# Attention scores computed a second time with keys on partitions, instead of transposing the exponentials

## The reference, cut to what matters

```python
q, k, v = (proj(Wq, bq), proj(Wk, bk), proj(Wv, bv))
scores = jnp.einsum('bhqd,bhkd->bhqk', q, k) / jnp.sqrt(jnp.float32(HD))
scores = scores + slopes[None, :, None, None] * distances[None, None, None, :]
scores = jnp.where(causal, scores, jnp.finfo(scores.dtype).min)
attn = jax.nn.softmax(scores, axis=-1)
ctx = jnp.einsum('bhqk,bhkd->bhqd', attn, v)
...
gate = jnp.einsum('bsh,ih->bsi', hidden_states, gate_w)
up = jnp.einsum('bsh,ih->bsi', hidden_states, up_w)
ffn = jnp.einsum('bsi,hi->bsh', silu(gate) * up, down_w)
out = x + (ctx @ Wo + bo) + ffn
```

## Time and profile before

| | us |
|---|---|
| device time, median of 3 runs (lowest, highest) | 875.54 (874.05, 877.53) |
| the profiled execution: its own time | 878.33 |
| the profiled execution: span of its instructions | 876.1 |
| TensorE busy | 712.3 (81%) |
| VectorE busy | 547.9 (63%) |
| ScalarE busy | 429.0 (49%) |
| GpSimd busy | 349.7 (40%) |

### The profile page before, as it was taken

How to read it: one execution, slowest core, us unless ns; L and a number is a source line. 1 busy time by engine, 2 the same in 40 slices (tenths; PEclk the granted TensorE clock), 3 DMA queues, 4 the chain that set the end, 5 groups by cost and what they waited for, 6 DMA issues and landing times. The chain is left out here.

```text
span 876.1 us, 15410 instructions
## 1 busy us (share of the span) xinstructions
PE 712.3 (81%) x4884; PEld 562.1 (64%) x4884; DVE 547.9 (63%) x1337; ACT 429.0 (49%) x961; POOL 349.7 (40%) x207
## 2 busy tenths in 40 slices
PE   5668878877788887798798778138896999999997
PEld 4556666665566665576576656026775888888886
DVE  5287879979779977969979884547532221321312
ACT  4257566657547756656856662124543233233331
POOL 2344434434334433435434441417314223524534
PEclk9878889999889998899999679657999999999999
DMA  7982374345375326365525941947435546524401
GB/s 243 216 191 38 86 149 117 44 79 88 85 192 74 48 50 118 77 170 73 74 51 119 232 171 64 328 130 241 112 117 166 164 130 214 168 73 132 144 1 49
DMA packets 53031, 109.90 MB, mean 125 GB/s; under 512 B 6360, under 2 KB 6616, under 8 KB 51416
## 3 DMA queue, kind: packets, MB, share of 16 engines
q1 hardware_dynamic: 52808, 108.82, 49.6%
q10 hardware_dynamic: 144, 0.07, 0.0%
HBM read 59.32 MB, written 25.17 MB: 96 GB/s over the span
## 5 line engine op out<-in xcount | busy, mean ns | idle before, releaser
L995 POOL TENSOR_TENSOR work<-work 128x1280 f16<-128x1280 f32 x64 | 168.1, 2626 | 263.1 <-DVE work L720 263.1
L908 ACT ACTIVATE work<-work,neg_max 128x128 f32<-128x128 f32 (+3 forms) x256 | 140.7, 551 | 183.6 <-DVE neg_max L713 183.6
L528 PE MATMUL bank<-ident,work 128*128 128x128 f16 x1280 | 115.1, 236 | 61.2 <-DVE work L727 56.6
L707 DVE CUSTOM_DVE_ANT_0 work<-bank,dist 128x128 f32<-128x128 f32 (+3 forms) x256 | 116.7, 488 | 67.3 <-PE bank L514 65.8
L1483 POOL TENSOR_TENSOR in_lo<-inner,in_hi 128x512 fp32r<-128x512 f32 x64 | 84.1, 1315 | 179.1 <-ACT in_hi L1386 179.1
L528 PEld LDWEIGHTS bank<-ident,work 128*128 128x128 f16 x1280 | 81.4, 106 | 108.4 <-DVE work L727 74.4
L1437 DVE TENSOR_TENSOR inner<-bank,silu 128x512 f32<-128x512 f32 x64 | 44.1, 689 | 134.3 <-ACT silu L1380 122.3
L1386 ACT CAST in_hi<-inner 128x512 fp32r<-128x512 f32 x64 | 39.7, 621 | 146.5 <-PE bank L1325 137.5
L917 ACT COPY work<-bank 128x768 f16<-128x768 f16 (+1 forms) x128 | 107.8, 891 | 2.8 <-PE bank L528 2.8
L514 PE MATMUL bank<-k_stack,q_stack 96*128 96x256 f32 (+2 forms) x256 | 80.8, 393 | 27.1 <-issue 9.4
L1323 PE MATMUL bank<-w_room,in_hi 128*128 128x512 f32 x256 | 100.4, 392 | 0.5 <-POOL in_lo L1483 0.5
(11 more groups left out here) (102 smaller groups left out, 1426.0 us busy)
## 6 DMA issues: line engine op xcount, KB each, us to landing
q_stack<-parts SPq DMA_DIRECT2D x48, 256.0 KB, 5.6
k_stack<-parts SPq DMA_DIRECT2D x48, 256.0 KB, 5.6
z<-xt_scratch SPq DMA_DIRECT2D x128, 88.0 KB
x_in<-x SPq DMA_DIRECT2D x32, 256.0 KB, 4.6
xt_scratch<-xt_room SPq DMA_DIRECT2D x8, 1024.0 KB, 6.5
xt_room<-xt_scratch SPq DMA_DIRECT2D x6, 1024.0 KB, 8.1
factor<-c_basis SPq DMA_DIRECT2D x5, 1024.0 KB, 10.9
taps<-windows SPq DMA_DIRECT2D x5, 1024.0 KB, 12.9
```

The lines of the kernel that those rows point to most:

```text
L528: mm = pe.transpose(pt_bank[i % 2][:, (part * n + k) * P:(part * n + k + 1) * P], probs16[:, s % 2, part, OFF[i] + k * P:OFF[i] + (k + 1) ...
L707: dve.tensor_tensor_reduce(probs[:, s % 2, OFF[i]:OFF[i] + n], score_bank[i % 2][:, 0:n], dist[:, S - n:S], 1.0, -3.4e38, ALU.add, ALU.max ...
L908: e = act.activation(tile, tile, ACT.Exp, bias=neg_max[:, s % 2, i:i + 1], scale=slope(s), accum_out=row_sum[:, s % 4, i:i + 1])
L995: pool.tensor_tensor(probs16[:, s % 2, 1, :], probs[:, s % 2, :], probs16[:, s % 2, 0, :], ALU.subtract).then_inc(lo_ready, 1)
```

## The change

The transposition of the exponentials is gone. Instead the scores are computed a second time with keys on partitions, so that their exponentials land transposed.

- VectorE's `bias_and_max` now keeps only the maxima (the biased scores go to a scratch tile `spill`). `negate_max`, VectorE's `probs_high` and both `take_turned` are removed.
- In the next step TensorE transposes the 128 x 4 maxima to 4 rows in the score bank (`turn_max`), ScalarE adds a shift and copies them to `max_rows` (`take_max`), and SP moves them as one row of 512 into row 97 (numbered from 1) of the head's `q_stack` (`load_max`). Rows 97 and 98 (`EDGE:ROWS`) of the stacks hold constants, set once by GpSimd at the start (two operations over 2 x 8 x 512) from a row of distances, so that the second product comes out as score + distance - maximum.
- Two steps after the first scores, `scores_t` computes the second ones in three units of 512, 384 and 384 columns (four float32r matmuls of 512, 384, 256 and 256 columns), each with a bfloat16 matmul of `ahead` by `ident16` of 128 columns that masks the diagonal block. ScalarE exponentiates from PSUM, three activations, no row sums; a step later it rounds to float16 (`probs_high`, now on ScalarE), GpSimd makes the rest, and `weigh_values` comes four steps after the scores. A value tile has two more columns that are one, so the product also holds the row sum.
- The stacks are rings of 8 heads. `stack` is per half of a group (two heads), four DMAs for each head: 8 for a half, 16 for a group, and now waits for both q and k first.
- The second scores of head s read a row that is there only after TensorE, ScalarE, SP and a DMA; and the second matmul of `scores` (i = 1) waits for `max_read`, since it writes the bank in which the maxima lie.
- The tables of units and turns are shifted by a step in places, and `load_early` is issued by ScalarE after step 12 of the last batch.

```diff
...
-OFF = [0, 128, 384, 768]
+ST_UNITS = 3
+ST_AT = [0, 512, 896]
+ST_COLS = [512, 384, 384]
+OFF = [0, 512, 896, 1152]
...
+RING = 8
+EDGE = 3 * HD
+ROWS = EDGE + 2
+ST_LAG, HALVE_LAG, AV_LAG = 2, 3, 4
...
-UNITS = {0: [("q", 1)], 1: [("k", 1)], 2: [("o", 0)], 3: [("o", 1)], 4: [("q", 2)], 5: [("k", 2)], 6: [("o", 2)],
+UNITS = {0: [("q", 1)], 1: [("k", 1)], 2: [("q", 2)], 3: [("o", 0)], 4: [("o", 1)], 5: [("k", 2)], 6: [("o", 2)],
...
-TURNS = {2: [("c", 3)], 7: [("c", 0)], 9: [("x", 0), ("x", 1)], 10: [("x", 2), ("x", 3)], 11: [("c", 1)],
-         15: [("c", 2)]}
...
-SPLITS = {13: [(0, 0)], 14: [(0, 1)], 1: [(0, 2)], 2: [(0, 3)], 4: [(1, 0)], 5: [(1, 1)], 6: [(1, 2)], 7: [(1, 3)]}
+TURNS = {0: [("c", 2)], 3: [("c", 3)], 8: [("c", 0)], 9: [("x", 0), ("x", 1)], 10: [("x", 2), ("x", 3)],
+         12: [("c", 1)]}
...
+                if h % 2 == 0 and i == 0:
+                    for m in range(2):
+                        pe.wait_ge(stacked[m][c % 2][h // 2], 2 * STACK * b + STACK * (c // 2 + 1))
...
+                if i == 1 and (later(b) or s >= 1):
+                    pe.wait_ge(max_read, H * b + s)
...
-            def turn_probs(b, s, i):
...
+            def turn_max(b, s):
+                pe.wait_ge(t_done, 64 * b + 4 * s + 4)
+                pe.transpose(score_bank[s % 2][0:QT, 0:P], row_max[:, s % 2, :], ident[:]).then_inc(max_full, 1)
+
+            def scores_t(b, s, u):
+                g = ST_UNITS * s + u
+                if u == 0:
...
-                    pe.wait_ge(hi_ready, H * b + s + 1)
-                    pe.wait_ge(lo_ready, H * b + s + 1)
-                if later(b) or 2 * s + i // 2 > 0:
-                    pe.wait_ge(pt_free[i % 2], 2 * (H * b + s) + i // 2)
-                n = i + 1
-                for part in range(2):
-                    for k in range(n):
-                        mm = pe.transpose(pt_bank[i % 2][:, (part * n + k) * P:(part * n + k + 1) * P],
...
+                    pe.wait_ge(max_ld[s % 2], 8 * H * b + 16 * (s // 2 + 1))
+                if later(b) or g >= 2:
+                    pe.wait_ge(p_ready, ST_UNITS * H * b + g - 1)
+                bank, slot = st_bank[g % 2], s % RING
+                if u == 2:
+                    pe.matmul(bank[:, P:3 * P], k_stack[:, slot, 3 * P:], q_stack[:, slot, 2 * P:], start=True,
+                              stop=False)
+                    pe.matmul(bank[:, 2 * P:3 * P], ahead[:], ident16[:], start=False, stop=True)
+                n = S - u * P
+                pe.matmul(bank[:, 0:n], k_stack[:, slot, u * P:(u + 1) * P], q_stack[:, slot, u * P:], start=True,
+                          stop=False)
+                pe.matmul(bank[:, 0:P], ahead[:], ident16[:], start=False, stop=True).then_inc(st_full, 1)
...
+                own, before, crossed, weighed = (back(b, s, n) for n in (0, 1, ST_LAG, AV_LAG))
...
+                early, rest = ([], units) if s == 4 else (units[:1], units[1:])
+                if before:
+                    turn_max(*before)
                 for i in range(2):
                     if own:
                         scores(b, s, i)
+                if crossed:
+                    scores_t(*crossed, 0)
                 for i in range(2):
                     if weighed:
                         weigh_values(*weighed, i)
...
-                for i in range(2, QT):
-                    if own:
-                        scores(b, s, i)
-                if turned:
-                    turn_probs(*turned, 0)
+                if own:
+                    scores(b, s, 2)
+                if crossed:
+                    scores_t(*crossed, 1)
+                if own:
+                    scores(b, s, 3)
                 for key in early:
                     unit(b, s, key, (2,))
-                if turned:
-                    turn_probs(*turned, 1)
+                if crossed:
+                    scores_t(*crossed, 2)
                 for i in range(2, QT):
                     if weighed:
                         weigh_values(*weighed, i)
-                for key in early if s != 2 else []:
+                for key in early if s != 3 else []:
                     unit(b, s, key, (3,))
-                for i in range(2, QT):
-                    if turned:
-                        turn_probs(*turned, i)
...
                 if (later(b) or s >= 2) and tiles[0] == 0:
-                    dve.wait_ge(lo_ready, H * b + s - 1)
...
-            def negate_max(b, s):
-                dve.wait_ge(t_done, 64 * b + 4 * s + 4)
-                dve.tensor_scalar(neg_max[:, s % 2, :], row_max[:, s % 2, :], -slope(s), None,
-                                  ALU.mult).then_inc(nm_ready, 1)
...
-            def probs_high(b, s):
-                dve.wait_ge(p_ready, H * b + s + 1)
-                if later(b) or s >= 2:
-                    dve.wait_ge(pt_full, 4 * (H * b + s - 1))
-                dve.tensor_copy(probs16[:, s % 2, 0, :], probs[:, s % 2, :]).then_inc(hi_ready, 1)
...
-            def take_turned(b, s, i):
-                n = 2 * (i + 1) * P
-                dve.wait_ge(pt_full, 4 * (H * b + s) + i + 1)
-                if i == 0 and (later(b) or s >= 2):
-                    dve.wait_ge(av_full, H * b + s - 1)
-                dve.tensor_copy(probs_t[:, s % 2, 2 * OFF[i]:2 * OFF[i] + n],
-                                pt_bank[i % 2][:, 0:n]).then_inc(pt_free[i % 2], 1)
...
+            def take_max(b, s):
+                act.wait_ge(max_full, H * b + s + 1)
...
+                if later(b) or s >= 2:
+                    act.wait_ge(max_ld[s % 2], 8 * H * b + 16 * (s // 2))
+                act.activation(max_rows[:, s % 2, :], score_bank[s % 2][0:QT, 0:P], ACT.Identity, bias=shift[:, 0:1],
+                               scale=1.0).then_inc(max_read, 1)
+
+            def probs_high(b, s):
+                act.wait_ge(p_ready, ST_UNITS * H * b + ST_UNITS * (s + 1))
+                if later(b) or s >= 2:
+                    act.wait_ge(av_full, H * b + s - 1)
+                act.copy(probs16[:, s % 2, 0, :], probs[:, s % 2, :]).then_inc(hi_ready, 1)
+
             def exponentials(b, s):
-                act.wait_ge(nm_ready, H * b + s + 1)
...
-                for i in range(QT):
-                    tile = probs[:, s % 2, OFF[i]:OFF[i] + (i + 1) * P]
-                    e = act.activation(tile, tile, ACT.Exp, bias=neg_max[:, s % 2, i:i + 1],
-                                       scale=slope(s), accum_out=row_sum[:, s % 4, i:i + 1])
-                e.then_inc(p_ready, 1)
-
-            def take_turned(b, s, i):
-                n = 2 * (i + 1) * P
-                act.wait_ge(pt_full, 4 * (H * b + s) + i + 1)
...
-                         pt_bank[i % 2][:, 0:n]).then_inc(pt_free[i % 2], 1)
+                if later(b) or s >= 2:
+                    act.wait_ge(lo_ready, H * b + s - 1)
+                for u in range(ST_UNITS):
+                    g = ST_UNITS * s + u
+                    act.wait_ge(st_full, ST_UNITS * H * b + g + 1)
+                    act.activation(probs[:, s % 2, ST_AT[u]:ST_AT[u] + ST_COLS[u]], st_bank[g % 2][:, 0:ST_COLS[u]],
+                                   ACT.Exp, scale=slope(s)).then_inc(p_ready, 1)
...
-                turned = back(b, s, 2)
-                if s < H:
-                    exponentials(b, s)
-                if turned:
-                    take_turned(*turned, 2)
-                    take_turned(*turned, 3)
+                before, crossed, halved = (back(b, s, n) for n in (1, ST_LAG, HALVE_LAG))
+                if before:
+                    take_max(*before)
+                if halved:
+                    probs_high(*halved)
+                if crossed:
+                    exponentials(*crossed)
...
+            edge = spill[EDGE:ROWS, 0:S].unsqueeze(1).broadcast_to([2, RING, S])
+            pool.tensor_copy(k_stack[EDGE:ROWS, :, :], edge).then_inc(edges, 1)
+            pool.tensor_scalar(q_stack[EDGE:ROWS, :, :], edge, 0.0, 1.0, ALU.mult, ALU.add).then_inc(edges, 1)
...
+            def stack(b, c, half):
+
+                for m in range(2):
                     sp.wait_ge(ql_ready, 8 * b + 2 * c + m + 1)
                     sp.nop(nofuse=True)
-                    for role, low in enumerate(((0, 1, 0), (0, 0, 1))[m]):
-
...
+                for h in (2 * half, 2 * half + 1):
+                    n = HPC * c + h
+                    if later(b) or n >= RING:
+                        sp.wait_ge(st_full, ST_UNITS * H * b + ST_UNITS * (n - RING + 1))
+                        sp.nop(nofuse=True)
...
+            def load_max(b, s):
+                sp.wait_ge(max_read, H * b + s + 1)
+                sp.nop(nofuse=True)
+                sp.dma_start(q_stack[EDGE:EDGE + 1, s % RING, :].bitcast(F32), max_rows[:, s % 2, :].bitcast(F32)
+                             ).then_inc(max_ld[s % 2], 16)
...
-                stack(b - 1, 3)
+                load_max(b - 1, 8)
+                load_max(b - 1, 9)
+                stack(b - 1, 3, 0)
```

(23 more changed lines are left out.)

232 lines of the change are left out of this document (128 added, 104 removed).

## The result

The changed kernel takes **929.5 us** (median of 4 runs, 922.7 to 931.2) against 876.5 for the kernel before beside it (4 runs): ratio 1.059, 95% interval 1.053 to 1.066. I had predicted 866 us and a range of 845 to 892. It is slower by 53 us, outside the range and on the other side of the forecast.

A forecast was written before the change was run, and what follows sets the result against it. It took VectorE to pace light steps and TensorE heavy ones. A 121.5 us pass against 124.9 gave -10 for the loop; start +3, last eight steps -4 and tail +2 made -9 off 875.54: 866 us, range 845 to 892.

The forecast's parts named there:

- TensorE's work, 86 us: Loop pass at full clock: 16 x 2.4 for scores, masks and values, 44 for units, 3.2 for x and context transposes.
- nothing worth naming: TensorE per head: 1.1 us of transposes removed against 0.64 second scores, 0.22 masks and 0.1 transpose added; negligible difference.
- The hand-off, 9.6 + 10.8 a pass: Second score matmul waits for ScalarE's take_max: 0.6 us every step, 1.35 more in eight steps with q or k projections.
- The clock, 3.4 a pass: TensorE's half-clock loss per pass, keeping only stretches after the loop's edge and in the x steps: 3.4 us.
- Rival B: TensorE's clock falls at hand-off gaps, five more per pass at 1.7 us each: +25, so 891 us; chance 0.20.
- VectorE freed, 2.8 us a head: VectorE loses negate_max, the rounding and two copies, about 2.8 of 6.5 us; busy near 60 us a pass.
- x chain, 4.5: Steps 8 to 10: next batch's x loads behind more SP work, so TensorE waits about 4.5 us a pass.
- Stacks and SP's queue, 1.0 a pass: Keys' stacks take 14.5 us until needed two steps later; 1.0 us is missing at one of four groups.
- rival D: SP's queue bounds: 80 small DMAs per pass, stacks 2 us later at four groups: +24, 890 us; chance 0.13.
- Start, +3 (-2 to +8): Before the loop: two new GpSimd operations, and the first maxima and stacks queued behind the 2944 KB copy: +3 us.
- Last eight steps, -4 (-8 to +1): Batch 3's end: steps without projections need about 4 us instead of 6.3, but steps 10 and 11 await stacks: -4.
- Tail, +2: Behind the last head: a fourth step, its maxima DMA and seven ScalarE DMA issues, against less work per step: +2.

The follow-up runs named there:

- e4: Kernel before, with only the four negated maxima moved from VectorE to ScalarE: 855.8 us, ratio 0.973 to the kernel before.
- e1: Changed kernel, with the transposed maxima put in a bank of the second scores instead of a score bank: 899.2 us, ratio 1.020 to the kernel before.
- e2: Changed kernel plus 28 matmuls of 128 columns in each of eight steps a pass, behind q or k projections: 900.0 us, ratio 1.026 to before.
- e9: Changed kernel with maxima transposed a step earlier (891.1 us), plus a semaphore for each head's stack DMAs: 890.8 us.
- e3: Changed kernel, with the 2944 KB bases copy issued on SP's queue behind the first eight rows of maxima: 922.1 us, ratio 1.051 to before.
- e11: Changed kernel with maxima transposed a step earlier (891.1 us), plus bases and zero copies issued on ScalarE's queue: 889.0 us.

## Why the prediction was wrong, point by point

**The sum was right in kind and set against the wrong thing.** This is the step that failed first. I added up the new pass from parts, 121.5 us, and compared it with a measured pass of before, 124.9. Made for the third pass of before, the same sum is 86 + 19.4 of idle time + 6 of clock = 111, where 123.0 were measured. So 12 us that the method does not see were credited to the change. Set against 111, my own 121.5 says +10 a pass, and with the terms outside the loop about 906 for the kernel. Against the 136.9 us that a pass took on average, the sum was 10.6 short on work and 10.6 short on the clock, and had 5.8 too much idle time.

**TensorE's work, 86 us: too low, by as much in both kernels.** Head by head the parts were taken from columns. In steps with one projection, full clock and no idle time, a step takes 5.57 us in the form before (e4, above). In the new form, e1 has two such steps in a row, of 5.48 and 5.60 (TensorE busy 11.00 of 11.00 us from 464.20 on, clock 1.00):

```profile
464.17 0.49 PE L524 MATMUL bank<-k_stack,q_stack 96*128 96x256 f32 x2
...
469.65 0.48 PE L524 MATMUL bank<-k_stack,q_stack 96*128 96x256 f32 x2
...
475.25 0.37 PE L524 MATMUL bank<-k_stack,q_stack 96*128 96x256 f32 x1
```

With 3.2 for the x and context transposes that is 16 x 5.57 + 3.2 = 92 before, and 91 to 93 after. Part of what was missing shows in any unit, whose first matmul behind small ones costs 0.32 between starts and not 0.23, in both forms:

```profile
355.04 0.48 PE L484 MATMUL bank<-xt_room,w_room 128*128 128x512 f32 x1
355.36 0.39 PE L485 MATMUL bank<-xt_room,w_room 128*128 128x512 f32 x1
355.59 0.40 PE L486 MATMUL bank<-xt_room,w_room 128*128 128x512 f32 x1
```

So "nothing worth naming" held for the difference between the forms, and the 0.64 in it too. What failed is the level, 86.

Other steps of the new form take longer with no gap listed, because a wait shorter than a matmul's drain passes as busy time. In e1's step of 5.84 us from 403.25, a start that comes 0.23 behind the one before it in the dense steps comes after 0.48:

```profile
406.75 0.40 PE L486 MATMUL bank<-xt_room,w_room 128*128 128x512 f32 x1
407.23 0.39 PE L546 MATMUL bank<-q_stack,k_stack 98*128 98x256 f32 x1
```

With 92 for the work, the third pass is 92 + 28.7 + 12 = 133 after, of 138.3, and 92 + 19.4 + 6 = 117 before, of 123.0: the same 5 to 6 us are missing in both. They lie within TensorE's busy time, since busy time by mean clock is 98 in both (103.8 x 0.94 and 109.9 x 0.89).

**The hand-off, 9.6 + 10.8 a pass: right mechanism, a little large.** It was TensorE's largest wait, as the prediction named, 16.4 us in the third pass (16.3 in the view). All idle time there was 28.7, and 26.3 on the average of the passes, against 32.1 in my sum (121.5 less 86 and 3.4). Plain steps had 0.33 to 0.7 for 0.6, steps behind q and k 1.6 to 2.0 for 1.8 to 2.2.

**The clock, 3.4 a pass: wrong, 12 in the third pass and 14 on average.** This is the mis-sized term that belongs to the change itself. Rival B had it, at a chance of 0.20, and sized its effect as +25 over the three passes; the count above has +23.7, and e2 got back 24 in them (3 x 7.9). I had laid the gaps of 1.8 to 2.2 between two rows of before (1.54 harmless, 2.48 harmful) and then taken the harmless side, even dropping some of what the kernel before already lost. Its bound for the mean clock, 0.88, was just not reached (0.89). The Trainium skill's page TensorE: Matmul & The Clock Gate, in "A second HAM failure mode: psum-queue depth-cycling", describes short idle times between groups of matmuls that make the clock go up and down; the trace agrees (gaps of 1.6 to 2.0 us, mean clock 0.89), and by it I should have put B first.

**VectorE freed, 2.8 us a head: 2.3 (106 to 70 us a pass, where I had named near 60), and worth less than it seemed.** e4 shows the part of it that mattered. Without `negate_max` on VectorE the kernel before gains 23 us; the changed kernel removed the same wait and lost more than this at its new one and to the clock. VectorE's busy share was the wrong thing to read; what TensorE waited for was one stall of VectorE, of 1.5 us per light step.

**x chain, 4.5: about right.** Waits for x and its low parts are 4.2 in the third pass, and before's were about 1. **Stacks and SP's queue, 1.0 a pass, rival D:** 1.4 in the third pass and less in the others, and e9 clears the queue in the loop.

**Start, +3 (-2 to +8): +8.5.** The two operations on GpSimd took 4.5 us each, near my lower value of 4.2, and step 0 began earlier than before. The mis-sized term was the first row of maxima behind the bases' copy, 8.9 us by itself; e3 and e11 show that it can be moved but hardly removed.

**Last eight steps, -4 (-8 to +1): +4.4** up to the start of step 15. One wait of 5.6 for the last stacks, as I had named it (steps 10 and 11), and gaps of 1.5 to 3.9 at a mean clock of 0.72. **Tail, +2: +2.9. Feed-forward, 0: +1.4.**

**What stays open.** Why one gap of 1.74 us is followed by half clock and the next of 1.74 by full is not settled. Nor is it shown whether short waits make up all of the 5 to 6 us a pass that no term and no listed gap holds, in either kernel.

## What to carry to other kernels

Compute a new stage's time by the same sum for the old stage first, and forecast from the differences; what the sum misses of the measured old stage belongs to both. Where a tuned kernel moves a reader from one engine to another, look at what stands ahead of the reader in that engine's order: TensorE waited not for 0.35 us of ScalarE but for everything before it. And look for an instruction whose duration is out of proportion to its shape: the 1.6 us for 128 x 4 was worth more, moved alone (23 us), than the redesign that also removed it.

## What I had not expected of the hardware

Adding 28 small matmuls in each of eight steps a pass made the changed kernel 29 us faster, with nothing else touched. And the VectorE-GpSimd exclusion moves with timing: taking it off a 128 x 4 operation (1337 to 208 ns, on ScalarE) put `normalize`'s multiplication from 292 to 571 ns, and taking a TensorE wait away in e1 made v's last operation 1078 ns in place of 426, up to 2.71 us at once. Such a cost can't be read off the trace of a kernel whose timing is about to change; only which operations are open to it can.
